# Perceiver block on one core: PE's second part inside both branches, and products of a constant ahead of five of its waits

## The chip, the cores and the metric

The kernel runs on one core of a Trainium2 chip. The metric is device time in microseconds (us) of one execution; before it is 1503.57 us, the median of three runs (1502.83 to 1508.02). The engines are PE (TensorE, with its weight loads shown as PEld), DVE (VectorE), ACT (ScalarE), POOL (GpSimd) and SP (SyncE, which here only issues DMAs). Each engine runs its own list of instructions in order, and the lists meet only through semaphores.

## The reference

A batch of 32 sequences of 64 tokens (2048 tokens, 256 features, kept transposed as x[feature, token]) goes through three residual steps:

```
x = x + cross_attention(layernorm(x), ctx, ctx, mask)   # 16 heads of 16, 1601 context rows per sequence
x = x + span_attention(layernorm(x))                    # 16 heads
x = x + ffn(layernorm(x))                               # a shared gated unit, and 8 experts, 2 for each token
```

The second step takes two numbers for each token and head from `h @ W_span.T`, a centre and a sharpness, and weighs the 64 positions with them:

```
mean = sigmoid(span[..., 0]) * m ;  soft = softplus(span[..., 1])
scores = -soft[..., None] * (pos - mean[..., None])**2
out = softmax(scores) @ (h @ W_val.T) ;  x = x + out @ W_out.T
```

The mask of this input holds ones only; the kernel must handle others too, for which it has a second version of part of its program.

## The kernel before

Each engine's program has three parts in a row. `queries` (the first 64 us) normalises x, projects the queries and prepares masks and weights. `cross_attention` runs over the 32 batches: in turn n PE computes scores and products of batch n and the keys, values and score maxima of batch n + 1. `tail` holds the rest: the output projection, the span step and the feed-forward step, over four chunks c of 512 tokens (8 sequences each), and then the routed experts.

**The branch.** The scores need an additional matmul for each tile if any mask element is 0. So PE's program of the turns exists twice. PE loads a number from the mask (`rows_all`, line 867) and compares it (line 868): `pe.If(rows_all < S)` holds `run(masked=True)`, a loop over the turns; `pe.Else()` holds `run(masked=False)`, all 31 turns written out, some 5,400 rows of PE's list. With a mask of ones the Else part runs. The other engines have no such branch.

**Head and body.** What PE does after the last turn is an order written out by hand, in two strings. `PE_HEAD` mixes the last batch's scores (`s0` to `s25`) and products (`p0` to `p10`, `l0`) with the first steps of the tail. `PE_BODY` holds all the others. A step is a letter and a chunk: `W` output projection of the cross attention (line 1417), `M`, `V` mean and variance of the first layernorm of the tail (lines 1449 and 1455, into `ln_bank[0]`), `m`, `v` those of the second, `S` the span product (line 1464, sixteen matmul records of 32 columns), `T` the turning of the packed span rows (line 1473), `A` one unit of distances (lines 1495, 1496), `X` values (1506), `U` sums (1514), `O` products (1523), `Z` output projection of the span step (1417 again), `F`, `G` the shared unit and `K`, `P` the experts (1531). `W0 W1 W2 M0 V0 S0 T0` stand in the head. `rest(pe)` returns both as functions: `rest_head` is called within `run`, in both branches, and `rest_body` once behind them.

**The waits that the change touches.** `S` for chunk c waits for `h_done`: ACT takes a logarithm from the bank (`lnv`, line 1143) and an exponential (1145), then DVE multiplies twice (`t_h`, line 1314). `V` waits for `sq_done`, ACT's square of what DVE has centred (`xc_done`, line 1303). `T` waits for `packed_done`, the end of nine dependent small DVE steps (lines 1325 to 1334) behind ACT's four on the span product. `mean_w` is a constant 128 x 128 tile (1/256 everywhere) made at the start; line 435 multiplies it with itself 18 times ahead of the first work.

**The start of batch 1.** In the first turn PE computes two chunks of keys of batch 1 (line 762), then scores of batch 0 (815), further keys, and score chunks of batch 1 (792). The last need the queries' rows of batch 1 (`qstack`, six DMAs of line 557) and a pair of its keys (`kstack`, line 564), all issued on SP's queue, there behind the load of the next context (545), which waits for the last `ctx_lo` of POOL (599).

Of the kernel before, what the change touches and what calls it, by code (L numbers as in the profile page):

```python
# [22 lines left out]
P = 128  # L23
B, S, S2, D = 32, 64, 1601, 256
# [416 lines left out]
def cross_attention(nc, sb, ins, bank, w, first_in, d, attn_out, out_done, q_parts, sem):  # L441
# [299 lines left out]
    def tensor(pe, early, rest):  # L741
# [60 lines left out]
        def scores(b, kt, h, masked):  # L802
            m = keys_of(kt)
            if kt == 0:
                pe.wait_ge(shift_done, 2 * b.n + h + 1)
                if h == 0 and isinstance(b.n, int) and b.n < 2:
                    pe.wait_ge(d["rows_in"][b.n], 16)

            need(pe, exp_done, NST * b.n + 2 * kt + h - 1)
            if masked:  # L810
                mask = w["mask_k"][0:m, kt, :].unsqueeze(1).to_broadcast([m, 2 * GROUPS, S])
                nc.tensor.matmul(st[h][0:m, :], w["ident_h"][0:m, 0:m], mask, start=True, stop=True, skip_group_check=True)
            for g in range(GROUPS):
                p = GROUPS * h + g
                mm = nc.tensor.matmul(st[h][0:m, g * PW:(g + 1) * PW], kstack[b.slot][0:KROWS, p, kt * P:kt * P + m],  # L815
                                      qstack[b.slot][0:KROWS, p, :], start=not masked and g == 0, stop=True, skip_group_check=True)
            mm.then_inc(st_ready, 1)
# [23 lines left out]
        def run(masked):  # L841
            def turn(cur, nxt, split, third):
                for kt in range(KT):
                    for what, i in slots[kt]:
                        if cur:
                            if what == "S":
                                scores(cur, kt, i, masked)
                            if what == "P":
                                products(cur, i)
                            if what == "L" and not first(cur):  # L850
                                products(before(cur), KT - 1)
                        if nxt:
                            if what == "K":
                                keys(nxt, i)
                            if what == "V":
                                values(nxt, i)
                            if what == "M":
                                chunk_scores(nxt, i)
                            if what == "T":
                                turn_shift(nxt)  # L860
            turns(pe, turn, loop=masked)
            rest_head({**last_products, "s": lambda i, _: scores(at(B - 1), i // 2, i % 2, masked)})


        rest_head, rest_body = rest(pe)
        last_products = {"l": lambda i, _: products(at(B - 2), KT - 1), "p": lambda kt, _: products(at(B - 1), kt)}
        rows_all = pe.value_load(w["rows_all"][0:1, 0:1], min_val=0, max_val=S)
        with pe.If(rows_all < S):
            run(masked=True)
        with pe.Else():  # L870
            run(masked=False)
        rest_body(last_products)

    return {"sync": sync, "vector": vector, "gpsimd": gpsimd, "scalar": scalar, "tensor": tensor}

# [12 lines left out]
def tail(nc, ins, bank, attn_out, out_done, wo, bo_all, mean_w, eps_col, ident, out_dram, d, sem):  # L888
# [6 lines left out]
    NC = NTOK // E  # L895
    FT = HS // P
    CLS = S // E

    PE_HEAD = """l0 s0 s1 s2 s3 p0 s4 s5 p1 s6 s7 p2 s8 p3 W0 s9 s10 s11 p4 s12 s13 M0 s14 s15 W1 s16 s17 V0 s18 s19 W2 S0 p5 p6 p7
        s20 p8 s21 s22 p9 s23 T0 s24 p10 s25"""  # L900
# [46 lines left out]
    with ExitStack() as own:  # L947
# [463 lines left out]
        def tensor(pe):  # L1411
            emitted = dict.fromkeys("WZFG", 0)

            def project(wt, src, done):
                for m in range(NK):
                    for k in range(NK):
                        i = nc.tensor.matmul(proj[m][:, :], wt[:, k, m * P:(m + 1) * P], src[k], start=k == 0, stop=k == NK - 1)
                i.then_inc(done, 1)
# [31 lines left out]
                i.then_inc(mean[j], 1)  # L1450

            def variances(c, j):
                pe.wait_ge(sq_done[j], c + 1)
                for k in range(NK):
                    i = nc.tensor.matmul(ln_bank[j][:, :], mean_w[:], sq[j][:, k, :], start=k == 0, stop=k == NK - 1)  # L1455
                i.then_inc(var[j], 1)

            def spans(c, _):
                if c == 0:
                    pe.wait_ge(s["w_in"], 4 * 16)  # L1460
                pe.wait_ge(s["h_done"], c + 1)
                for blk in range(BLOCKS):
                    for k in range(NK):
                        i = nc.tensor.matmul(ln_bank[0][:, 2 * H * blk:2 * H * (blk + 1)], h[c % 2][:, k, blk * P:(blk + 1) * P],
                                             wspan[:, k, :], start=blk == 0 and k == 0, stop=k == NK - 1, skip_group_check=True)
                i.then_inc(s["span"], 1)

            def turn_rows(c, _):
                if c == 0:
                    pe.wait_ge(s["turn_ready"], 2)  # L1470
                pe.wait_ge(s["packed_done"], c + 1)
                for blk in range(BLOCKS):
                    i = nc.tensor.matmul(ln_bank[0][:, blk * P:(blk + 1) * P], packed[:, blk, :], ident_r[:], start=blk == 0, stop=True,
                                         skip_group_check=True)
                i.then_inc(s["turned"], 1)
# [197 lines left out]
```

## Time and profile before

| what | value |
|---|---|
| median of three runs | 1503.57 us (1502.83 to 1508.02) |
| the profiled execution | 1506.76 us |
| its span, first to last instruction | 1504.9 us |
| busy: PE, PEld, DVE, ACT, POOL | 98%, 83%, 66%, 61%, 30% |
| mean granted clock of PE | 0.991 of 2.4 GHz |
| PE waited in S, T, V of line 1455 | 3.9, 2.2, 1.0 us |

The profile is of one execution. In order of time, a row gives the start, the duration, the engine, the line and what is written from what; behind it in brackets is the idle time of the engine before it and what released it, as inferred from semaphores. A row can gather several records of one kind. Durations of PE's records overlap, since matmuls are pipelined: the distance from one start to the next tells more than the duration. By stretch, the profile gives each engine's busy time and the granted clock, 1.00 for 2.4 GHz and 0.50 for 1.2 GHz.

### The profile page before, as it was taken

The page shows a single profiled execution, that of the slowest core. Times are in us where ns is not written, and L with a number is a line of the kernel's source. Part 1 is how long each engine was busy: PE and PEld are TensorE (multiplying, and loading weights), DVE is VectorE, ACT ScalarE, POOL GpSimd, SP SyncE. Part 2 cuts the span into 40 slices and gives each one's busy share as a digit, 9 for nine tenths or more (in the row PEclk, how much of TensorE's full clock was granted, in tenths as well). Part 3 has the DMA queues.
Part 4 walks back from the last instruction along what each step waited for, and adds up shares of the span by engine and source line. Part 5 has one row for each costly group of instructions (what it writes and reads, how often), then busy time and mean ns, then how long its engine had stood idle before and what let it go on. Part 6 is the DMA issues. An engine that isn't in the chain of part 4 may idle for free. (4 is left out here: it accounts for less than half of the span.)

```text
span 1504.9 us, 56291 instructions
## 1 busy us (share of the span) xinstructions
PE 1469.9 (98%) x23456; PEld 1251.7 (83%) x23456; DVE 1000.3 (66%) x3958; ACT 922.0 (61%) x1827; POOL 450.2 (30%) x564
## 2 busy tenths in 40 slices
PE   9899999999999999999999999999999999999999
PEld 5688888888888888888888888888888885555698
DVE  5766666676666677676676667666667774655436
ACT  4366666665666666666666666666666664689583
POOL 5433333333333333333333333333333303001143
PEclk9999999999999999999999999999999999899999
DMA  5634444444344444444444444444444333000012
GB/s 179 185 101 103 115 116 109 118 118 120 101 120 116 112 119 118 111 117 108 116 121 116 103 117 117 105 117 118 115 117 117 89 104 122 1 1 9 21 57 85
DMA packets 91758, 156.24 MB, mean 104 GB/s; under 512 B 44896, under 2 KB 55904, under 8 KB 91488
## 3 DMA queue, kind: packets, MB, share of 16 engines
q1 hardware_dynamic: 91216, 151.57, 37.3%
q8 instruction: 189, 3.10, 0.9%
q0 software_dynamic: 288, 1.05, 0.2%
q14 instruction: 65, 0.53, 0.1%
HBM read 69.61 MB, written 4.19 MB: 49 GB/s over the span
## 5 line engine op out<-in xcount | busy, mean ns | idle before, releaser
L682 DVE CUSTOM_DVE_ANT_0 junk<-bank,mask_q 128x400 bf16<-128x400 f32 (+1 forms) x1024 | 547.5, 571 | 178.0 <-issue 171.9
L627 ACT ACTIVATE probs<-bank 128x512 f32<-128x512 f32 (+1 forms) x832 | 468.3, 596 | 124.1 <-PE bank L815 115.3
L596 POOL CAST ctx_hi<-ctx_raw 128x400 fp32r<-128x400 f32 x248 | 123.0, 525 | 782.2 <-PE bank L772 782.2
L815 PE MATMUL bank<-qstack,kstack 104*128 104x128 f16 (+1 forms) x3328 | 289.1, 220 | 1.2 <-ACT probs L627 1.0
L772 PE MATMUL bank<-wv_hi,ctx_hi 128*128 128x256 f32 (+1 forms) x832 | 280.2, 337 | 0.0
L671 DVE SCALAR_TENSOR_TENSOR k_lo<-bank,bk,k_hi 128x400 f16<-128x400 f32 (+1 forms) x256 | 162.0, 633 | 161.6 <-ACT k_hi L637 161.5
L647 ACT ACTIVATE v<-bank 128x256 f32<-128x256 f32 (+1 forms) x416 | 159.6, 384 | 178.6 <-PE bank L772 172.3
L792 PE MATMUL bank<-kstack,qstack 96*128 96x400 f16 (+1 forms) x1024 | 266.9, 336 | 2.0 <-issue 1.3
L815 PEld LDWEIGHTS bank<-qstack,kstack 104*128 104x128 f16 (+1 forms) x3328 | 214.7, 99 | 61.3 <-issue 18.3
L637 ACT ACTIVATE k_hi<-bank,bk 128x400 f16<-128x400 f32 (+1 forms) x256 | 152.3, 595 | 177.9 <-PE bank L762 169.9
L599 POOL TENSOR_TENSOR ctx_lo<-ctx_raw,ctx_hi 128x400 fp32r<-128x400 f32 x248 | 253.6, 1043 | 0.0
L772 PE MATMUL bank<-wv_lo,ctx_hi 128*128 128x256 f32 (+1 forms) x832 | 233.4, 281 | 0.0
L772 PE MATMUL bank<-wv_hi,ctx_lo 128*128 128x256 f32 (+1 forms) x832 | 232.0, 279 | 0.0
L832 PE MATMUL bank<-probs,v 128*32 128x64 f32 x13312 | 221.6, 221 | 6.5 <-issue 5.9
L832 PEld LDWEIGHTS bank<-probs,v 128*32 128x32 f32 x13312 | 198.8, 110 | 21.6 <-issue 12.9
L762 PE MATMUL bank<-ctx_hi,wk_hi 128*128 128x400 f32 (+1 forms) x512 | 191.0, 373 | 4.6 <-POOL ctx_lo L599 4.5
L762 PE MATMUL bank<-ctx_hi,wk_lo 128*128 128x400 f32 (+1 forms) x512 | 177.3, 346 | 0.0
L762 PE MATMUL bank<-ctx_lo,wk_hi 128*128 128x400 f32 (+1 forms) x512 | 176.9, 345 | 0.0
L772 PEld LDWEIGHTS bank<-wv_hi,ctx_hi 128*128 128x128 f32 (+1 forms) x832 | 154.4, 186 | 5.7 <-issue 0.5
L772 PEld LDWEIGHTS bank<-wv_lo,ctx_hi 128*128 128x128 f32 (+1 forms) x832 | 154.4, 186 | 0.0
L772 PEld LDWEIGHTS bank<-wv_hi,ctx_lo 128*128 128x128 f32 (+1 forms) x832 | 153.5, 184 | 0.0
L792 PEld LDWEIGHTS bank<-kstack,qstack 96*128 96x128 f16 x1024 | 81.8, 98 | 48.1 <-issue 16.8
(172 smaller groups left out, 1642.0 us busy)
## 6 DMA issues: line engine op xcount, KB each, us to landing
ctx_raw<-in_ctxT SPq DMA_DIRECT2D x32, 1602.0 KB, 6.9
kstack<-k_hi SPq DMA_DIRECT2D x512, 100.1 KB, 2.2
kstack<-k_lo SPq DMA_DIRECT2D x256, 100.1 KB, 2.2
weight<-in_w SPq DMA_DIRECT2D x18, 256.0 KB, 2.7
x<-in_xT SPq DMA_DIRECT2D x8, 512.0 KB, 9.1
qstack<-q_parts SPq DMA_DIRECT2D x192, 16.0 KB, 5.2
out_yT<-y SPq DMA_DIRECT2D x8, 256.0 KB, 2.9
weight<-in_sw SPq DMA_DIRECT2D x3, 512.0 KB, 6.3
```

The source lines that it names most:

```text
L596: nc.gpsimd.tensor_copy(c_hi[:, k, s0:s0 + n], raw[:, k, s0:s0 + n]).then_inc(ctx_hi, 1)
L599: nc.gpsimd.tensor_tensor(c_lo[:, k, s0:s0 + n], raw[:, k, s0:s0 + n], c_hi[:, k, s0:s0 + n].bitcast(F32), ALU.subtract).then_inc(ctx_lo, 1)
L627: nc.scalar.activation(probs[kt % NP][0:m, GROUPS * h:GROUPS * (h + 1), :], st[h][0:m, :], ACT.Exp, scale=DK ** -0.5 / (UP * UP)).then_inc ...
L637: nc.scalar.activation(k_hi[:, t, s0:s0 + n], pj[(b.slot + c) % 2][:, 0:n], ACT.Identity, bias=w["bk"][:, t:t + 1]).then_inc(khi_done, 1)
L647: nc.scalar.activation(heads, pj[(b.slot + NCK + i) % 2][0:m, 0:D].rearrange("s (p e d) -> s p e d", e=2, d=DK), ACT.Copy).then_inc(v_done, 1)
L671: nc.vector.scalar_tensor_tensor(k_lo[:, t, s0:s0 + n], pj[(b.slot + c) % 2][:, 0:n], w["bk"][:, t:t + 1], k_hi[:, t, s0:s0 + n], ALU.add, ...
L682: nc.vector.tensor_tensor_reduce(junk[i % SM][:, 0:n], sm[i % SM][:, 0:n], w["mask_q"][:, s0:s0 + n], 1.0, -3.0e38, ALU.add, ALU.max, part ...
L762: mm = nc.tensor.matmul(o, w[wp][:, k, t * P:(t + 1) * P], cp[:, k, s0:s0 + n], start=i == 0, stop=i == len(terms) - 1)
L772: mm = nc.tensor.matmul(o, cp[:, k, j * P:j * P + m], w[wp][:, k, :], start=i == 0, stop=i == len(terms) - 1)
L792: nc.tensor.matmul(sm[i % SM][:, 0:n], qstack[b.slot][0:KSTACK, p, :], kstack[b.slot][0:KSTACK, p, s0:s0 + n], start=True, stop=True).then ...
L815: mm = nc.tensor.matmul(st[h][0:m, g * PW:(g + 1) * PW], kstack[b.slot][0:KROWS, p, kt * P:kt * P + m], qstack[b.slot][0:KROWS, p, :], sta ...
L832: mm = nc.tensor.matmul(ob[32 * g:32 * g + 32, t * S:(t + 1) * S], v[b.slot][0:m, kt, c0:c0 + 2 * DK], probs[kt % NP][0:m, p, S * e:S * (e ...
```

## The change

Three things, all on PE. `rest_body` moves from behind the two branches into `run`, so that both branches hold head and body. The branches are exchanged: the comparison is now `rows_all == S`, with the unmasked program first and the masked one in the Else. And a table `KEEP` puts products of `mean_w` with itself, 128 columns each, ahead of five waits: 7 before span product S0, 4 before variance V1 (chunk 1 of the first norm), 9 before T1, 3 before S2 and 6 before S3. They write into a bank that is free there and that the awaited step writes next (for T into `proj[1]`), and each is preceded by a wait of its own that makes the bank free.

```diff
             rest_head({**last_products, "s": lambda i, _: scores(at(B - 1), i // 2, i % 2, masked)})
+            rest_body(last_products)
...
-        with pe.If(rows_all < S):
+        with pe.If(rows_all == S):
+            run(masked=False)
+        with pe.Else():
             run(masked=True)
-        with pe.Else():
-            run(masked=False)
-        rest_body(last_products)
...
+    KEEP = {("S", 0): 7, ("V", 1, 0): 4, ("T", 1): 9, ("S", 2): 3, ("S", 3): 6}
...
+            def keep_going(where, dst):
+
+                for _ in range(KEEP.get(where, 0)):
+                    nc.tensor.matmul(dst[:, 0:P], mean_w[:], mean_w[:], start=True, stop=True)
...
             def variances(c, j):
+                if ("V", c, j) in KEEP:
+                    pe.wait_ge(xc_done[j], c + 1)
+                    keep_going(("V", c, j), ln_bank[j])
                 pe.wait_ge(sq_done[j], c + 1)
...
             def spans(c, _):
...
+                if ("S", c) in KEEP:
+                    pe.wait_ge(lnv[0], c + 1)
+                    keep_going(("S", c), ln_bank[0])
                 pe.wait_ge(s["h_done"], c + 1)
...
             def turn_rows(c, _):
...
+                if ("T", c) in KEEP:
+                    proj_free(1)
+                    keep_going(("T", c), proj[1])
                 pe.wait_ge(s["packed_done"], c + 1)
```

PE's list around the branch before, as laid out in memory. The first rows behind the comparison are the masked program (its line 812 is the additional matmul); the unmasked one begins behind the jump of line 868:

```order
L800 MATMUL bank<-turn_down,row_max 8x128
L867 TENSOR_LOAD rows_all
L867 ISA x2
L868 COMPARE_AND_BRANCH
```

```order
L812 MATMUL bank<-mask_k,ident_h 65x512
L815 MATMUL bank<-qstack,kstack 65x128 x4
L868 UNCONDITIONAL_BRANCH
L762 MATMUL bank<-ctx_hi,wk_hi 128x400
L762 MATMUL bank<-ctx_hi,wk_lo 128x400
L762 MATMUL bank<-ctx_lo,wk_hi 128x400
```

And now, where the row behind the comparison belongs to the unmasked program, and the jump at that program's end leads over the masked one:

```order
L868 TENSOR_LOAD rows_all
L868 ISA x2
L869 COMPARE_AND_BRANCH
L762 MATMUL bank<-ctx_hi,wk_hi 128x400
L762 MATMUL bank<-ctx_hi,wk_lo 128x400
```

```order
L1546 MATMUL bank<-gelu_lo,w_0_hi 128x256
L1546 MATMUL bank<-gelu_hi,w_0_lo 128x256
L869 UNCONDITIONAL_BRANCH
L762 MATMUL bank<-ctx_hi,wk_hi 128x400
L762 MATMUL bank<-ctx_hi,wk_lo 128x400
```

So the target of the taken path moved from some 1,700 rows away to the next row, and the far jump from the start to the end.

PE around S0 before (in the unmasked program; 1417 is W2, 1464 the span product, 832 the products of batch 31):

```order
L1455 MATMUL bank<-t_sq,mean_w 128x512 x2
L815 MATMUL bank<-qstack,kstack 128x128 x8
L1417 MATMUL bank<-attn_out,wo 128x512 x4
L1464 MATMUL bank<-wspan,t_h 128x32 x8
L832 MATMUL bank<-probs,v 32x64 x48
```

and now (1423 is W2, 1418 the constant products, 1476 the span product):

```order
L1464 MATMUL bank<-t_sq,mean_w 128x512 x2
L815 MATMUL bank<-qstack,kstack 128x128 x8
L1423 MATMUL bank<-attn_out,wo 128x512 x4
L1418 MATMUL bank<-mean_w 128x128 x7
L1476 MATMUL bank<-wspan,t_h 128x32 x8
L832 MATMUL bank<-probs,v 32x64 x48
```

Nothing else stands in a new place there; seven rows came in between W2 and S0. The same holds at T1, before:

```order
L1495 MATMUL bank<-rows,sel_a 128x512
L1496 MATMUL bank<-rows,sel_b 128x512
L1473 MATMUL bank<-ident_r,packed 128x128 x4
L1495 MATMUL bank<-rows,sel_a 128x512
L1496 MATMUL bank<-rows,sel_b 128x512
```

and now, with nine products between the two units A0 and T1 (line 1488):

```order
L1510 MATMUL bank<-rows,sel_a 128x512
L1511 MATMUL bank<-rows,sel_b 128x512
L1418 MATMUL bank<-mean_w 128x128 x9
L1488 MATMUL bank<-ident_r,packed 128x128 x4
L1510 MATMUL bank<-rows,sel_a 128x512
L1511 MATMUL bank<-rows,sel_b 128x512
```

A row here is one matmul of the program; the trace shows two records for a plain float32 one, hence sixteen for S. PE's list has one more change: the body, some 780 rows, stands in both branches, so the masked program moved and the whole is that much longer.

## Rows read from the trace of the kernel before

**Rows 1.** The page, section 1: busy us, share of the span, instructions.
```profile
PE 1469.9 (98%) x23456; PEld 1251.7 (83%) x23456; DVE 1000.3 (66%) x3958; ACT 922.0 (61%) x1827; POOL 450.2 (30%) x564
```

**Rows 2.** PE in order of time: start us, us, engine, line, work.
```profile
68.37 0.67 PE L762 MATMUL bank<-ctx_hi,wk_hi 128*128 128x400 f32 x1 [4.47 <-POOL ctx_lo L599]
...
80.59 0.68 PE L792 MATMUL bank<-kstack,qstack 96*128 96x400 f16 x3
```

**Rows 3.** PE's sequencer, line 868: the branch; ns, and its start.
```profile
L868 PEldq COMPARE_BRANCH  x1: 3824/3824/3824, 64.4 to 64.4; - x1
```

**Rows 4.** DMA queues in 63 to 69 us: packets, MB, share.
```profile
q8 instruction: 1, 0.02, 1.0%
```

**Rows 5.** One stretch: us; PE, PEld, DVE, ACT, POOL busy; clock; DMA.
```profile
65.14:71.97 6.83, 3.60 (x11) 3.60 (x12) 0.59 (x2) 0.59 (x1) 4.22 (x5) 0.50 0.41 136
```

**Rows 6.** The SP queue, 68 to 77 us, and the last landings of L557.
```profile
68.44 3.61 SPq L557 DMA_DIRECT2D qstack<-q_parts  x6
76.56 0.51 SPq L564 DMA_DIRECT2D kstack<-k_hi  x1
...
DMA to landing us min/median/max: 4.4/4.6/4.7
```

**Rows 7.** Four stretches of the end; columns as in rows 5.
```profile
1263.22:1270.04 6.82, 6.82 (x154) 6.02 (x157) 2.43 (x10) 2.98 (x8) 0.00 (x0) 0.50 0.09 29
...
1287.11:1293.94 6.83, 5.24 (x11) 3.35 (x12) 4.24 (x13) 4.81 (x10) 0.00 (x0) 0.50 0.00 0
...
1307.59:1311.00 3.41, 3.41 (x7) 1.65 (x6) 3.13 (x11) 1.88 (x5) 0.00 (x0) 0.50 0.00 0
...
1331.48:1334.90 3.42, 3.42 (x95) 3.35 (x98) 0.00 (x0) 2.21 (x6) 0.00 (x0) 0.50 0.02 7
```

**Rows 8.** PE in order of time, 1262 to 1300 us; columns as in rows 2.
```profile
1262.14 2.61 PE L1464 MATMUL bank<-wspan,t_h 128*128 128x32 f32 x16 [1.77 <-DVE t_h L1314]
...
1264.68 2.79 PE L832 MATMUL bank<-probs,v 128*32 128x64 f32 x96
...
1271.54 0.65 PE L832 MATMUL bank<-probs,v 128*32 128x64 f32 x32
...
1272.38 1.94 PE L1449 MATMUL bank<-x,mean_w 128*128 128x512 f32 x4
...
1276.78 1.99 PE L1455 MATMUL bank<-t_sq,mean_w 128*128 128x512 f32 x4 [0.96 <-ACT t_sq L1136]
...
1288.70 1.11 PE L1473 MATMUL bank<-ident_r,packed 128*128 128x128 f32 x4 [2.08 <-DVE packed L1334]
...
1291.43 3.13 PE L1449 MATMUL bank<-x,mean_w 128*128 128x512 f32 x4
```

**Rows 9.** PE, continued, 1302 to 1345 us.
```profile
1302.59 1.99 PE L1523 MATMUL bank<-attn_out,vbd 128*32 128x64 f32 x128 [0.34 <-ACT vbd L1193]
1305.20 1.97 PE L1464 MATMUL bank<-wspan,t_h 128*128 128x32 f32 x16 [0.62 <-DVE t_h L1314]
...
1308.38 4.90 PE L1417 MATMUL bank<-rs,wout 128*128 128x512 f32 x8
...
1330.19 2.47 PE L1464 MATMUL bank<-wspan,t_h 128*128 128x32 f32 x16 [1.48 <-DVE t_h L1314]
1332.59 3.07 PE L1523 MATMUL bank<-attn_out,vbd 128*32 128x64 f32 x128
...
1341.02 3.67 PE L1417 MATMUL bank<-rs,wout 128*128 128x512 f32 x8
```

**Rows 10.** Products of the constant with itself, 128 columns, at the start.
```profile
1.56 5.33 PE L435 MATMUL bank<-mean_w 128*128 128x128 f32 x24
...
7.11 0.98 PEld L435 LDWEIGHTS bank<-mean_w 128*128 128x128 f32 x8
```

**Rows 11.** Who waited on PE, and PE's sequencer at the block's end.
```profile
PE bank L832 <- issue: 5.9, 6, 1.4
...
L156 PEldq DRAIN  x1: 2345/2345/2345, 1499.2 to 1499.2; - x1
```

## The prediction, made before the changed kernel ran

> **What bounds the kernel now.** I read the page first: PE is busy for 1469.9 us of 1504.9 [rows 1]. Such a share says that PE sets the pace, not that it runs well: a matmul at half clock is busy too. So the next two views were PE in order of time (where does it stand idle?) and the busy time by stretch, whose clock column is what the throttle granted. In both the reader is to look at the same two places, because the long middle (batches 1 to 31, from the first scores to batch 31) has next to no idle time on PE, full clock, and no line of this diff but its place in memory.
>
> The first place is the branch. After PE's last instruction of the first part it stands idle for 4.47 us [rows 2]. The row names POOL's ctx_lo as the releaser. I don't believe it: the first keys product waits for the first chunk's ctx_lo of batch 1, and POOL splits the chunks in order, so it was the last chunk, not the first, that ended just then. The sequencer's row has the cause: the compare and branch of line 868 starts at 64.4 us and takes 3.824 us [rows 3], and one block of instructions (0.02 MB) is fetched meanwhile [rows 4]. In the kernel before, the masked part stands first and this input (a mask of ones) jumps over it. PE then comes back at half clock: 0.50, the 1.2 GHz level, from 65.14 to 71.97 us [rows 5].
>
> The second place is the end. Four stretches, of 6.8, 6.8, 3.4 and 3.4 us, run at 0.50 [rows 7]. Each begins at, or a microsecond or a few after, one of the waits of this diff: the span product S0 after 1.77 us idle, T1 (packed rows) after 2.08 [rows 8], S2 after 0.62 and S3 after 1.48 [rows 9]. Ahead of each fall stood idle time and the sixteen 32-column matmuls of a span product. V1 waits 0.96 us [rows 8] with no fall behind it.
>
> **Part 1, the branch turned round.** PE's instructions stay the same; the unmasked part now follows the comparison directly. Removed: a jump of 3.82 us. What a comparison that falls through costs, no row shows; it lies between nothing and the same 3.82 us. I take 0.1, since what the long row holds is the fetch, and the block that follows needs none that isn't under way. So PE could start its keys at about 64.7 rather than 68.37, and as it stood idle for 0.8 us only, at full clock: of the half-clock stretch, 3.6 us were work [rows 5], which shrink to about 1.8. That is 3.7 + 1.8 = 5.5 us at the end of the first keys.
>
> It isn't kept whole. The first score chunk of batch 1 ran at 80.59 [rows 2] and would now be due at 75.1. It needs the queries' rows, six DMAs issued on SP from 68.44 to 72.05, of which the last lands 4.7 us after its issue, at 76.3 [rows 6]. Their start hangs on POOL's last ctx_lo, which the change doesn't touch. Behind them on the same queue comes the first pair's k_hi: it was issued at 76.56, when its keys were done; now its keys are done at 71, it goes out at 72.1, and its three DMAs end about 77. So the new wait is on this chunk, some 1.9 us, and 80.59 becomes about 77.1: **3.5 us gained** (bounds: none, if falling through costs like the jump, and 5.5). From there PE sets the pace again.
>
> The Trainium skill (Runtime: NRT & Kernel Launch, section Instruction fetch mechanics) says that a taken branch to a target outside the fetched window waits for a DMA of that page, and the trace agrees: 3.824 us and one fetch. By Advanced Engine Details and Errata of the Trainium skill, section Control Flow Timing, a compare-and-branch is about 108 ns; by that figure the sum would be the same within 0.1 us.
>
> The same cost comes back at the end: the unmasked part now closes with a jump over the masked one. PE's sequencer runs ahead of its matmuls; it entered the drain at 1499.2 and waited there for 2.345 us [rows 11]. A jump of 3.8 us started then is over at 1503.0, ahead of the span's end at 1504.9, which the last store sets. So I cost it at nothing, with some 1.9 us of cover; without any cover it costs 3.8. The jump at the old join goes; no idle time stands there, so it gives nothing.
>
> **Part 2, the constant products.** Twenty-nine products mean_w times mean_w, 128 columns, two matmul records each. The kernel already issues 18 such at its start: records at the first, slow pace take 5.33/24 = 0.22 us, those at the later pace 0.98/8 = 0.12 with the tail, about 0.112 without [rows 10]. A product costs 0.22 us at full clock and 0.43 at half. So S0 gets 7 x 0.22 = 1.6 us in a wait of 1.77, V1 0.9 in 0.96, T1 2.0 in 2.08, S2 0.7 in 0.62, S3 1.3 in 1.48: 6.5 us in 6.9, each about as long as its wait. At full clock they cost nothing: the cover is the idle time, and what ends it (t_h, packed, t_sq) comes from DVE and ACT. The waits put ahead of them are on events long past: the logarithm for S, the centred chunk for V, the free bank for T. Nothing is queued behind them that could have gone earlier, as PE is in order.
>
> What they bring is the clock. If it stays at 2.4 GHz through all four stretches, the gain is the work in them at full pace, each compared with the same form at full clock:
> - A (S0): the span product 2.61 against 1.97 us, the three products of batch 31 2.79 against 3 x 0.65 [rows 8, 9], and some 2.6 us of smaller pieces to about 1.5: 0.6 + 0.85 + 1.1 = 2.6.
> - B (T1): the means 3.13 against 1.94; T1 and two units, 1288.70 to 1291.43, to about 1.7 [rows 8]: 2.2. The next centring stands behind 16 small bias steps on DVE, so I take 2.0 (1.2 to 2.5).
> - C (S2): the output projection 4.90 against 3.67 [rows 9]: 1.3 with the units.
> - D (S3): 2.47 against 1.97, and 3.07 against 1.99 [rows 9]: 1.5.
>
> Sum 7.4 us. No wait is expected to take its place: within A to D, DVE and ACT wait for PE, and what follows up to the end is PE's shared and routed products, which just start earlier.
>
> **The sum.** The profiled execution took 1506.8 us (span 1504.9 and 1.9 around it), 3.2 above the median of the runs. 1506.8 - 3.5 - 7.4 = 1495.9. If the 3.2 us are the profile's cost, it would be 1492.7; if the median run had fewer half-clock stretches, they aren't there to be won and 1495.9 stands. I take **1495.0**. One more unknown: moved code meets other block boundaries. PE's six idle pieces ahead of line 832 with no releaser, 5.9 us [rows 11], look like late fetches in dense small matmuls; they can come out 2 us either way.
>
> **Rivals.**
> 1. The clock falls all the same (17%). For it: the sixteen 32-column matmuls behind each wait stay, and V1 shows that idle time alone doesn't decide. Against: idle time stood ahead of all four falls. It gives 1503.6 - 3.5 = 1500.1, up to 1503. The Trainium skill (TensorE: Matmul & The Clock Gate, section Why this matters for your kernels) warns only of idle gaps longer than any of these; by that rule filling them would give nothing, which is this rival. The trace disagrees: the clock fell behind gaps of 0.62 to 2.08 us.
> 2. Falling through costs what the jump did (10%): 1495.0 + 3.5 = 1498.5.
> 3. Slower (5%): the products themselves run at half clock. Place: S0 to S3, if the clock has fallen before PE gets there. Price: 29 x 0.43 = 12.4 us against 6.9 of waits, 5.5 over; from 19 products at half clock on they outlast the waits by more than the start gives back. With the end jump uncovered as well: 1503.6 + 5.5 + 3.8 - 3.5 = 1509.4.
>
> **How the numbers follow.** Both gains hold: 68%, 1490.5 to 1499. Under 0.5%, 7.5 us, a measurement of this kernel can't be told from no change; the border is 1496.05. Of the 68, 57 lie under it; 3 more come from rivals 1 and 2 with the other part larger: faster 0.60. Slower by over 0.5% needs rival 3 nearly whole: 0.03. The rest is 0.37. The range 1490 to 1500.5 takes in the 68, rival 2 and the best part of rival 1.
>
> **What would show it.** Line 869's branch in well under 0.5 us; the first score chunk at 76.5 to 77.5 behind a wait of 1 to 2.5 us; clock 1.00 at 65 us and from 1260 to 1335; M1's means start about 6 us earlier than 1272.4; a fetch behind the end jump that ends ahead of the last store. Wrong would be: 3.8 us at the fall-through, 0.50 behind S0 or T1, or products that end after t_h.

## The result: no gain, and the profile after

| | before | changed |
|---|---|---|
| median | 1504.28 us (20 runs, 1497.8 to 1511.7) | 1509.42 us (20 runs, 1504.5 to 1513.5) |
| ratio, 95% interval | 1 | 1.0024 (1.0013 to 1.0036) |
| profiled execution, span | 1506.76, 1504.9 us | 1508.69, 1506.9 us |
| mean granted clock, profiled / mean of runs | 0.991 / 0.994 (35 later runs) | 0.996 / 0.996 |

Forecast were 1495.0 us and a range of 1490 to 1500.5. The mechanisms that the forecast named came as it said, and yet the kernel is 0.24% slower: a small loss, but clear of its interval.

Page of the changed kernel, section 1, to be read beside [rows 1], and the branch on PE's sequencer (ns, first and last start), beside [rows 3]:

```profile
PE 1472.2 (98%) x23514; PEld 1254.3 (83%) x23514; DVE 999.8 (66%) x3958; ACT 920.8 (61%) x1827; POOL 450.5 (30%) x564
...
L869 PEldq COMPARE_BRANCH  x2: 88/1890/3693, 64.6 to 1500.8; - x2
```

The comparison that falls through takes 88 ns at 64.6 us; the far jump, 3693 ns, now stands at 1500.8. PE in order of time, beside [rows 2] (start us, us, engine, line, work, idle time before it):

```profile
64.89 0.42 PE L762 MATMUL bank<-ctx_hi,wk_hi 128*128 128x400 f32 x1 [0.73 <-issue]
...
77.36 0.67 PE L792 MATMUL bank<-kstack,qstack 96*128 96x400 f16 x3 [1.65 <-DMA qstack<-q_parts]
```

The first keys start at 64.89 rather than 68.37, the first score chunk of batch 1 at 77.36 rather than 80.59 (77.1 was forecast), behind the new wait for the queries' rows (1.65 us, forecast 1.9).

Stretches of the changed kernel by busy time and clock, columns as in [rows 5]:

```profile
78.73:82.14 3.41, 3.41 (x105) 3.19 (x107) 0.59 (x5) 1.03 (x3) 0.00 (x0) 0.50 0.70 161
1239.26:1242.67 3.41, 3.41 (x76) 2.76 (x68) 2.73 (x6) 1.72 (x4) 1.74 (x3) 0.50 1.01 364
1263.22:1270.04 6.82, 6.81 (x207) 5.97 (x207) 3.86 (x12) 4.11 (x11) 0.00 (x0) 1.00 0.15 42
1287.11:1293.94 6.83, 6.52 (x28) 3.52 (x32) 4.89 (x20) 5.24 (x13) 0.00 (x0) 1.00 0.00 0
...
1368.96:1372.37 3.41, 3.41 (x6) 1.45 (x6) 3.37 (x6) 2.54 (x4) 0.00 (x0) 0.50 0.00 0
```

The four half-clock stretches of [rows 7] are gone. Three shorter ones are new: one right behind the new wait, one at 1239 us, one at 1369 us. (Three kernels among the experiments have one at 1238 to 1240 us too, with and without the products; what brings it stays open.) The constant products fill their waits (line 1418), and what follows runs at full pace, beside [rows 8]:

```profile
1261.80 1.72 PE L1418 MATMUL bank<-mean_w 128*128 128x128 f32 x14
1263.48 1.97 PE L1476 MATMUL bank<-wspan,t_h 128*128 128x32 f32 x16
1265.38 1.55 PE L832 MATMUL bank<-probs,v 128*32 128x64 f32 x96
...
1287.18 0.66 PE L1488 MATMUL bank<-ident_r,packed 128*128 128x128 f32 x4
...
1289.02 1.96 PE L1455 MATMUL bank<-x,mean_w 128*128 128x512 f32 x4
```

What came on top is in the list of who waited, beside [rows 11] (us in total, times, longest; "issue" is idle time for which the profile shows no releaser), and in PE's order at the first O product, beside [rows 9]:

```profile
PE bank L832 <- issue: 5.9, 6, 1.8
PE bank L1538 <- issue: 4.7, 4, 1.7
...
PE bank L762 <- issue: 1.7, 2, 1.0
PE bank L792 <- DMA qstack<-q_parts: 1.6, 1, 1.6
...
PE bank L792 <- issue: 1.5, 3, 0.7
```

```profile
1300.17 1.95 PE L1538 MATMUL bank<-attn_out,vbd 128*32 128x64 f32 x122 [0.90 <-ACT vbd L1194]
1303.80 0.31 PE L1538 MATMUL bank<-attn_out,vbd 128*32 128x64 f32 x6 [1.68 <-issue]
```

An O product is 128 small matmuls that wait once, at their start. Now PE stands still six matmuls before the end of it, for 1.68 us, released by nothing that the profile shows. The DMA view of 1300 to 1304 us (40 slices of 0.1 us) has a single packet, an instruction block, which begins in the slice of 1301.4 us, 2.4 us before PE goes on:

```profile
DMA  0000000000000050000000000000000000000000
...
q8 instruction: 1, 0.02, 1.4%
```

I then numbered all of PE's records from the start of the trace, its loads and those of its sequencer included (a semaphore wait is a record too; without them the pattern is lost), and looked at each idle piece without a releaser in the middle (from 76 us on) and in the O products. In the kernel before, 7 of 10 stand at remainder 144 or 145 of 256, in the changed one 7 in the middle and all 4 in the O products at 193 or 194; these end 2.2 to 2.9 us after a fetch has begun. The others, at line 792, stand at other remainders and end 3.2 to 3.7 us behind a fetch. There are 189 fetches of 16384 bytes for 48,047 records, one for every 256. I read the pieces at one remainder as block boundaries whose block isn't there yet.

Start times of the changed kernel less those of the profiled kernel before, record by record: -3.2 us at 80.6, -1.7 at 83.8 (half clock), -3.9 at 420, +0.5 at 1212, +1.6 at 1256, -1.5 at 1272 (S0), -2.4 at 1302 (T1), -0.4 at 1305 (late fetch in O0), -2.2 at 1313 (S2), -3.2 at 1341 (S3), 0.0 at 1376 (late fetch in O2 and the half clock behind it), +1.5 at 1405 (O3), +2.0 at the end. So this execution lost 3.3 us in the middle (83.8 to 1256 us) and gained nothing from there on, where 7.4 us were forecast.

### The profile page after: what moved, and what is told of

Its sections match the earlier page's. It is cut to its first block and busy times, and to the rows that moved or that the text cites. A ratio compares the mean times of both kernels' runs of the same rounds, so it can differ in the third digit from the quotient of the medians.

```text
span 1506.9 us, 56408 instructions
## 1 busy us (share of the span) xinstructions
PE 1472.2 (98%) x23514; PEld 1254.3 (83%) x23514; DVE 999.8 (66%) x3958; ACT 920.8 (61%) x1827; POOL 450.5 (30%) x564
```

## The experiments

The theory, called P (placement) from here: the change moved code in memory, and late instruction blocks in PE's dense small matmuls ate what branch and clock gave. The rivals: the gains weren't there, or the products or the end jump cost time. Each ratio is against the kernel before on the same chip. "Place" in the table is the remainder of 256 at which the middle's late fetches stand, counted over the records that all kernels share; the middle's idle time is that without a releaser ahead of lines 762, 772, 792 and 832, in the one profiled execution, without two pieces of another kind: 0.7 us behind the branch in the changed kernel and e10, and 0.6 us that is left of the wait for the queries' rows in e6. O0 to O3 are the O products of chunks 0 to 3.

| run | ratio, 95% interval | mean clock | place | idle, middle | idle, O |
|---|---|---|---|---|---|
| before | 1 | 0.994 | 144 | 7.2 | 0 |
| changed | 1.0024 (1.0013 to 1.0036) | 0.996 | 193 | 8.4 | 4.7 |
| e1 | 0.9995 (0.9977 to 1.0012) | 0.998 | 77 | 11.1 | 0 |
| e2 | 1.0050 (1.0035 to 1.0065) | 0.992 | 77 | 10.8 | 0 |
| e3 | 0.9987 (0.9971 to 1.0004) | 0.995 | 193 | 7.4 | 0 |
| e4 | 1.0012 (0.9997 to 1.0028) | 0.996 | 117 | 8.5 | 0 |
| e5 | 0.9992 (0.9980 to 1.0004) | 0.998 | 193 | 7.6 | 0 |
| e6 | 0.9975 (0.9963 to 0.9987) | 0.999 | 165 | 5.0 | 0 |
| e7 | 1.0028 (1.0014 to 1.0042) | 0.996 | 193 | 7.3 | 4.8 |
| e8 | 0.9997 (0.9984 to 1.0009) | 0.997 | 144 | 7.1 | 0 |
| e9 | 1.0008 (0.9993 to 1.0023) | 0.995 | 144 | 10.8 | 1.6 |
| e10 | 1.0020 (1.0007 to 1.0032) | 0.996 | 193 | 5.9 | 1.9 |
| e11 | 1.0003 (0.9987 to 1.0019) | 0.998 | 165 | 6.8 | 0 |
| e12 | 1.0002 (0.9990 to 1.0015) | 0.999 | 153 | 8.9 | 0 |
| e13 | 0.9955 (0.9940 to 0.9971) | 0.999 | 165 | 6.1 | 0 |
| e14 | 0.9988 (0.9973 to 1.0004) | 0.997 | 144 | 5.7 | 0 |
| e15 | 0.9979 (0.9968 to 0.9991) | 0.998 | 193 | 5.5 | 0 |

**e1, the changed kernel with other places.** 29 small products (116 records) ahead of the branch.

```diff
+        for _ in range(29):
+            nc.tensor.matmul(ob[0:32, 0:S], w["turn_down"][:, 0:32], w["turn_down"][:, 0:S], start=True, stop=True)
         rows_all = pe.value_load(...)
```

> The changed kernel with 29 tiny products (32 x 64 columns, four records each, 116 in all, about 1 us) between the last step of the first part and the load of rows_all. They do no work that is needed. They lie ahead of the wait of the first score chunk of batch 1, which was 1.65 us, so they should cost nothing. Theory P (placement): in the traces of before and after, PE's idle pieces without a releaser lie, counted in PE's executed records, all at one remainder of 256: 144 before, 193 after, and end 2.3 to 2.9 us behind the fetch of an instruction block. After pays 4.7 us of them within the four O steps, before none. 116 records more bring the remainder to 77: the O stalls go (4.7 to under 0.5 us), the half-clock stretch behind O2 at 1369 us (1.3 us) with them, the middle stays at 9 to 10 us of stalls. So 5 to 6 us below the changed kernel, equal to or up to 2 us under before. Rival R (the constant products or the exchanged branches cost it elsewhere): as the changed kernel, or 1 us slower by the added products.

The O products have no idle piece left and the median is 1502.77 us, 0.3% under the changed kernel by the ratios. The middle was worse (one piece of 3.2 us at 1242 us, half clock there). The 29 products took 3.4 us, not 1; they push the keys into the new wait, and there is no half clock behind it here. So e1 changes two things at once, and the O products alone are for e5 and e15.

**e2, dead code alone.** The kernel before with 17 small products (68 records) at the head of the masked program, which never runs.

```diff
         with pe.If(rows_all < S):
+            for _ in range(17):
+                nc.tensor.matmul(ob[0:32, 0:S], w["turn_down"][:, 0:32], w["turn_down"][:, 0:S], start=True, stop=True)
             run(masked=True)
```

> The kernel before with 17 tiny products (68 records) at the head of the masked branch, which this input never executes; it stands ahead of the unmasked one in memory. Every executed instruction is as before, 68 places further on. Theory P: the remainder goes from 144 to 76, a block boundary then falls 200 to 250 records into each of the four O steps (their first records are at 124, 84, 84 and 123): about 4 us of stalls there, and the middle goes from 7.4 to about 9.3 us. In sum 4 to 6 us slower than before. Rival R: dead code costs nothing, the time is that of before.

Who waited on PE in e2:

```profile
PE bank L832 <- issue: 8.4, 7, 2.1
...
PE bank L792 <- issue: 1.8, 4, 0.6
```

1510.46 us, 1.0050. The late fetches moved from remainder 144 to 76 and 77, by the 68 records. PE executes the same instructions; that places alone move the time is thereby shown. But the 4 us that were expected in the O products didn't come: they have no idle piece. By the start differences of its profiled execution the loss lies in the middle: -0.1 us at 83.8, +7.0 at 1256. Of that, 3.6 us are idle time; two half-clock stretches at 1162 and 1247 us, each right behind a late fetch, can be most of the rest. e1, at the same place, lost 7.0 us in the middle as well.

**e3 and e4, one part of the change each.** e3 is the changed kernel with `KEEP = {}`; e4 the kernel before with `KEEP` and its three `if ... in KEEP` blocks.

> The changed kernel without any constant product (an empty table). Theory P: the start keeps its 3.2 us, the middle loses 2.5 (9.9 against 7.4 us of stalls), one half-clock stretch behind the first score chunk of batch 1 costs 1.3, the remainder 193 meets no O step at its end (they start at 124, 84, 84, 123), and the four half-clock stretches of before are back. So within 1.5 us of before, 3 to 5 us below the changed kernel. Rival R1 (the exchanged branches are what costs): as the changed kernel or slower, as the clock's gain of 7.6 us is gone: 1511 to 1516.

> The kernel before with the constant products alone: branches in the old order, the second part behind them. Theory P: PE's start is as before (3.8 us in the branch), the middle keeps its 7.4 us of stalls and remainder 144; the clock stays at 1.00 from 1260 to 1335 us, which brings 7 us or so; the O steps now start at 204, 200, 200, 239, so that the boundary at 144 lies 161 to 200 records into them, where a stall of 0 to 1 us each is possible. In sum 3 to 7 us faster than before. Rival R2 (the products are the loss): 2 to 5 us slower than before.

e3 held in kind: the branch alone gives 0.9987, 2 us, a little more than expected (its interval reaches 1.0004), and far from a loss through the exchanged branches. e4 missed: the products alone give nothing in the median, although its profiled execution (span 1499.7) shows all four stretches at full clock. The seven products of S0 stand in the masked program too, so the place moved by 28 records, to 117, and the middle's idle time rose from 7.2 to 8.5 us. That left the clock term open. Neither has an idle piece in the O products: the loss needs both parts of the change.

e3 shows more. Its profiled execution has no product in any wait, and still its clock stayed at 1.00 at S0 and S2, behind waits of 1.07 and 0.62 us; it has two half-clock stretches from 1260 to 1340 us (1286 and 1327), 3.4 us each, where the profiled kernel before has four with 20.5 us.

**e5, only the O products moved.** The changed kernel, with T1's nine products replaced by five and 29 small ones, which puts all behind T1 100 records further on.

```diff
-    KEEP = {..., ("T", 1): 9, ...}
+    KEEP = {..., ("T", 1): 5, ...}
...
                     keep_going(("T", c), proj[1])
+                    for _ in range(29):
+                        nc.tensor.matmul(proj[1][0:32, 0:64], mean_w[:, 0:32], mean_w[:, 0:64], start=True, stop=True)
```

> The changed kernel, with only the place of the tail's code moved: ahead of T1 stand 5 constant products of 128 columns and 29 of 64 columns by 32 in place of the 9, so everything behind T1 lies 100 matmul and load records further on in PE's list; nothing ahead of it moves. Placement theory (the four idle pieces of the O products are fetches of instruction blocks that come late because a block boundary falls 210 to 249 records into each O): the boundary now falls some 110 to 149 into each, the idle time within them goes from 4.7 us to under 0.5, the middle's idle pieces stay at one record in 256 as in the changed kernel, and the median is 3 to 6 us under the changed kernel's, 1.000 to 1.002 of the kernel before. Rival (the O products wait for data, values or unit sums that the constant products delay): the 4.7 us stay within 1 us and the time with them, 1.0024 or more.

The idle 4.7 us are gone and the ratio falls from 1.0024 to 0.9992, by 4.8 us (3 to 6 expected). The O products didn't wait for data. Nor did this filler come free. PE around T1 in e5:

```profile
1281.90 1.28 PE L1418 MATMUL bank<-mean_w 128*128 128x128 f32 x10
1283.10 3.43 PE L1487 MATMUL bank<-mean_w 128*32 128x64 f32 x58
1286.46 0.66 PE L1490 MATMUL bank<-ident_r,packed 128*128 128x128 f32 x4
```

4.5 us of products stand in a wait of 2.1: T1 starts 2.3 us late by start differences. This overrun sits in e5, e6, e8, e11 and e12 alike.

**e6, the new wait filled too.** e5 and seven products of `turn_down` with itself ahead of the first score chunk of batch 1.

```diff
+            if i == 0 and isinstance(b.n, int) and b.n == 1:
+                need(pe, *((shift_done, 2 * b.n) if SHIFT_BANK == 0 else (sm_done, NMX * b.n)))
+                for _ in range(7):
+                    nc.tensor.matmul(sm[0][:, 0:P], w["turn_down"][:], w["turn_down"][:], start=True, stop=True)
             if i == 0:
                 pe.wait_ge(qstack_in[b.slot], 16 * QSTACK_DMAS * b.used)
```

> The kernel of the run before, and 7 products of a constant (128 columns) in the wait ahead of the first score chunk of batch 1. If the half-clock stretch at 78.7 us in the changed kernel comes from the new wait of 1.65 us, the clock stays at 1.00 there and the run gains a further 1 to 1.5 us of it; the middle's code lies 28 records further on, so its idle pieces come elsewhere, 2 us either way. Expected 0.996 to 1.001 of the kernel before. If the stretch comes whatever is in the wait, it is there again and the products cost up to 0.3 us.

No half clock at 78 us, and from 80.6 to 83.8 us nothing is lost, where the changed kernel loses 1.5 us; ratio 0.9975. The middle's place moved too, which e11 takes apart.

**e7, the end jump.** The changed kernel without `with pe.Else(): run(masked=True)`; the masked program is left out.

> The changed kernel without its masked program (which this input never runs; masks with zeros would be computed wrongly), so the jump at the end of PE's program leads to the next row instead of far ahead. What is executed ahead of the jump stays at its place. If the end jump of 3.69 us is covered, as the prediction had it, the time is that of the changed kernel within 1.5 us, with the same idle pieces at record 193 of 256. If the run's end waits for it, it is 2 to 3.7 us faster (0.998 to 0.9995 of before where the changed kernel is 1.0024).

```profile
L869 PEldq COMPARE_BRANCH  x1: 87/87/87, 62.6 to 62.6; - x1
```

The jump of 3.7 us is gone, and the ratio is 1.0028, no faster than with it: the jump was covered. The late fetches stayed, in the O products too (4.8 us).

**e8, e4 with the places held.** e4 with T1 as in e5 and 57 small products (228 records) of dead code, so that 28 + 228 = 256.

> The kernel before with the constant products alone (five waits, T1 filled as in the first run of this group), the branch as it was, and with 228 records of code that never runs put into the masked program, so that the middle's block boundaries fall at the same records as in the kernel before (144 of 256; 117 in the run with the products alone) and those of the O products at 80 to 130 records into each. Placement theory: the products' gain by the clock stands alone, the mean granted clock goes from 0.994 to 0.996 or 0.997, the median is 2.5 to 4.5 us under the kernel before, ratio 0.997 to 0.9985, and the middle's idle pieces are those of the kernel before (7 us). Rival (the products cost as much as the clock gives, since they outlast their waits): ratio 1.000 to 1.002, as with the products alone.

The place is 144 again, as meant. At 0.9997 the gain of 0.0015 to 0.003 was missed, and the overrun at T1 explains 2.3 us of it.

**e9 and e10, how sharp the distance is.** e9 is the kernel before with 17 small products ahead of T1, e10 the changed kernel with two more there.

> The kernel before, with 17 products of 64 columns by 32 (68 records) executed ahead of T1, inside its wait of 2.08 us, and nothing else: the middle stays at its place (idle pieces at record 144 of 256), and the block boundaries fall 208, 248, 248 and 209 records into the four O products instead of 20, 60, 60, 21. Placement theory: idle pieces of 0.2 to 1.7 us come up inside the O products, 3 to 5 us in sum, where the kernel before has none, and the median is 2 to 5 us above it (1.0015 to 1.0035). Against it stands the run with 68 records of dead code, whose O products have the same distances to a boundary and no idle piece: if the distance alone doesn't decide, there is none here either and the time is that of the kernel before within 1 us.

> The changed kernel with two more small products (8 records) ahead of T1. The boundaries fall 237, 241, 241 and 202 records into the O products instead of 245, 249, 249, 210. If the late fetch is a matter of tens of records, the four idle pieces stay, 4 to 5 us in sum, at record 193 of 256, and the time is the changed kernel's within 1 us; if a few records decide whether a fetch starts ahead of the O product's wait or behind it, one or more of them is gone and the time is 1 to 4 us less.

e9 has one idle piece, in O2, and none in the three other O products, and 1.0008 where 1.0015 to 1.0035 was expected:

```profile
1368.30 1.98 PE L1527 MATMUL bank<-attn_out,vbd 128*32 128x64 f32 x124 [1.15 <-ACT vbd L1193]
1371.86 0.31 PE L1527 MATMUL bank<-attn_out,vbd 128*32 128x64 f32 x4 [1.58 <-issue]
```

So a boundary late in an O product makes the stall possible in the kernel before as well, but doesn't decide it. e10 lost two of its four for 8 records. In e2 the O products stand at the same distances as in e9, and their fetches began 0.9 to 2 us before the O products of chunks 1 to 3 started; in the changed kernel those that stalled them began 0.6 to 1.3 us after the start of chunks 0, 2 and 3. When a fetch begins relative to the wait ahead of it decides; what sets that moment stays open. e10's time fell by less (0.0004) than its 2.8 us of idle time; the intervals overlap, so its share isn't settled.

**e11 and e12, the fastest kernel taken apart.** e11 is e5 with seven small products ahead of the branch (e6's places, without its products at batch 1); e12 is e6 with three small ones there.

> The first run of the second group (the changed kernel with its O products shifted, 0.9992) with 7 small products (28 records) ahead of the branch, so that the code stands at the same places as in the fastest run so far (0.9975), but nothing fills the wait ahead of the first score chunk of batch 1. If the 2.1 us between those two came from the clock kept at 78 us, this one has a half-clock stretch there and a median 1 to 2 us above the fastest, 0.9985; if they came from the place of the middle's code, its idle pieces are 5 to 6 us here too and it is within 0.7 us of the fastest.

> The fastest kernel so far (changed kernel, O products shifted, 7 constant products ahead of batch 1's first score chunk) with 12 more records ahead of the branch: the middle's idle pieces then come at content 12 records earlier. Nothing that computes is changed. Placement theory: the idle pieces change in size and places, 5.3 us to anything from 4.5 to 10 us, and the time with their sum; ratio 0.9965 to 1.0005. Rival (the sum of idle pieces varies from run to run by as much, and place says nothing for so small a step): within 0.7 us of the fastest.

e11 has a half-clock stretch of 6.8 us at 76.4 us behind a wait of 3.5 us, and 1.0003 where 0.9985 was expected: direction right, size not; its stretch is twice as long as the changed kernel's and costs 2.6 us by start differences. e12 ran with mean clock 0.999 and yet gives 1.0002; its middle has 3.9 us more idle time than e6's. Three profiled executions at place 165 have 5.0, 6.8 and 6.1 us, e12's at 153 has 8.9. At one place the sum varies too, at 144 from 5.7 to 10.8 (the latter in e9, whose profiled execution is its slowest of twelve, 1511.9 us at a median of 1505.2), so one profile doesn't settle 12 records.

**e13 to e15, a filler that fits.** T1 gets four products of 128 columns and 50 of a cheaper form (one matmul record each instead of two), 116 records in all: in e13 on top of e6, in e14 on top of e8, in e15 on top of the changed kernel.

```diff
+    KEEP = {..., ("T", 1): 4, ...}
...
+                    for _ in range(50):
+                        nc.tensor.matmul(proj[1][0:32, 0:32], ident_r[:, 0:32], ident_r[:, 0:32], start=True, stop=True)
```

> The fastest kernel so far (changed kernel, O products shifted, 7 constant products ahead of batch 1's first score chunk; 0.9975) with a cheaper filler ahead of T1: 4 constant products of 128 columns and 50 single-pass products of 32 columns (116 records) in place of 5 and 29 double-pass ones, which took 4.5 us in a wait of 2.1. The O boundaries fall 137 to 141 and 102 records in. If the overrun of 2.3 us at T1, seen in five traces, is real, T1 starts as early as in the changed kernel, and the median is 2 to 2.5 us lower, ratio 0.995 to 0.997. If T1 waits on something else, it stays 0.9975.

> The kernel before with the constant products alone and places held (0.9997 with the expensive filler), now with the cheap one ahead of T1. It gives the price of the prediction's second term by itself: if the clock's gain is there and the filler ate it, ratio 0.997 to 0.999 and mean granted clock 0.997; if the term was mis-sized for a median run, which has a clock of 0.994 where the profiled one had 0.991, it is at the upper end of that, 0.998 to 0.999; if the products give nothing at all, 0.9995 or more.

> The changed kernel with nothing but its O products shifted, by the cheap filler (80 records; boundaries 165, 169, 169, 130 records in). The price of the four late fetches by themselves: expected 4.7 us less idle and no cost at T1, ratio 0.9965 to 0.9985 against 1.0024 for the changed kernel. If the changed kernel loses elsewhere, 0.9985 or more.

PE in e15, around T1 and at O0:

```profile
1280.68 1.05 PE L1418 MATMUL bank<-mean_w 128*128 128x128 f32 x8
1281.49 1.81 PE L1487 MATMUL bank<-ident_r 128*32 128x32 f32 x50
1283.15 0.64 PE L1490 MATMUL bank<-ident_r,packed 128*128 128x128 f32 x4
...
1295.93 1.99 PE L1540 MATMUL bank<-attn_out,vbd 128*32 128x64 f32 x128 [0.91 <-ACT vbd L1194]
```

The filler ends within 0.25 us of its wait, and O0's 128 matmuls run in one piece. All three came out as expected: e15 0.9979, e14 0.9988, e13 0.9955. e13 is 1497.15 us where the kernel before is 1503.81; by its ratio it beats both kernels. Its stretches from 76 to 80 and from 1262 to 1335 us (busy time, clock):

```profile
76.00:80.00 4.00, 3.74 (x146) 3.33 (x147) 1.58 (x9) 1.37 (x3) 0.00 (x0) 1.00 0.68 156
...
1262.00:1335.00 73.00, 71.09 (x731) 46.50 (x728) 43.73 (x104) 55.39 (x118) 0.00 (x0) 1.00 0.01 2
```

## Why the prediction was wrong, step by step

**The step that failed** is the last of the sum: "they can come out 2 us either way". It read the 5.9 us ahead of line 832 rightly as late fetches, but took the places in the middle for the only ones. The O products have none in [rows 9] and so had no row. They are 256 records in 2 us, as dense as line 832's. The turned branch moved the boundaries from 144 to 193, and the constant products push the O products along: 28 records from S0, 16 from V1, 36 from T1 and more behind. In O0 the boundary thereby moved from about 20 records in to about 245, close to its end. One part of the change alone leaves it at about 69 (e3) or 168 (e4), where no O product stalled. The term measured: 4.7 us idle in the O products, and 1.5 us by the half-clock stretch behind the stall, at 1369 us; the four executions that stalled in O2 (changed, e7, e9, e10) are the four that have a stretch there. By ratios the same kernel with these products moved (e15) is 1.0024 - 0.9979 = 0.0045, 6.8 us, faster, and at least 3.3 by the ends of the two intervals. In the traces the start differences from 1256 us to the last matmul are -7.4 us in e1, e13, e14 and e15, -7.5 in e4, and 0.0 in the changed kernel: 7.4 us. The middle doesn't show a share: at place 193 it idled 5.5 to 8.4 us in six executions, at 144 5.7 to 10.8 in four, and from 83.8 to 1256 us the start differences are -0.7 to +3.3 us (mean 1.8) in the six, -1.6 to +7.3 (mean 2.0) in the four. So the 3.3 us that the profiled execution lost there are within what one place gives.

This term isn't the whole miss. Without it the kernel would be at 0.9979, about 1501.1 us, still above the range's end of 1500.5. The gains forecast were 8.6 us, and 3.2 came (e15); the term that was too large is part 2's, below. The sign that it had named, M1's means about 6 us earlier than 1272.4, came as 1.5 us in the changed kernel, after the 3.3 us lost in the middle, and as 5.8 in e15.

**Part 1, the branch, was right.** 88 ns for the fall-through, 3.22 us at the first score chunk of 3.5, and the end jump covered (e7), though it starts 1.6 us later than thought, at 1500.8, and ends at 1504.5, ahead of the span's end at 1506.9. Left out was that the new wait brings a fall of the clock, as the waits of the end did: 1.5 us, from -3.2 to -1.7 at 83.8. e3, the branch alone, gives 2.0 us (0.9987). In e6, e12 and e13, with that wait filled, nothing is lost from 80.6 to 83.8 us. What the first part gives varies as well: the comparison starts anywhere from 62.6 to 64.9 us in the profiled executions without added products ahead of it, the two compared here at 64.4 and 64.6.

**Part 2, the clock, was right in the trace and too large for a median run.** By start differences A to D gave 3.1, 0.9, 1.8 and 1.1 us, 6.9 of 7.4; in e13 3.4, 1.1, 1.7 and 1.6. B is half of what was forecast; I didn't test why. But alone, with places held, the products give 1.8 us of median (e14, 0.9988, interval to 1.0004). One reason is in the clocks: (1 - 0.991) x 2 x 1505 = 27 us at half clock in the profiled execution, (1 - 0.9937) x 2 x 1502 = 19 in a mean run of the kernel before (0.989 to 0.998 in 35 runs). The prediction weighed that and took its profiled execution as the base all the same. With about 7 us of each at the branch, 12 instead of 20.5 us were there to be won at the end, some 4.3 us instead of 7.4 (an estimate). The traces say the same without that estimate: e2 and e3, which have no product in any wait, run the stretch from 1256 us to the last matmul 4.4 and 4.5 us faster than the profiled kernel before. Of the 7.4 us only 2.9 to 3.0 are left for the products against these two. The products themselves can cost a little: against the work ahead of it, S0 starts 0.3 to 0.5 us later than in e3, and the cheaper filler delays T1 by 0.2. The rest of the way to 1.8 lies within e14's interval.

**The rivals.** Rival 1 (the clock falls all the same) didn't come: 1.00 in all four stretches. The Trainium skill (TensorE: Matmul & The Clock Gate, section Why this matters for your kernels), which warns of longer gaps only, was rightly set aside. Of the 13 profiled executions with the products, 12 have no half-clock stretch from 1260 to 1340 us (e7 has one, behind a late fetch in O0), where the kernel before has four, e2 three, e3 two and e9, with a filler at T1 alone, one. Rival 2 is excluded by 88 ns. Rival 3 was the only case given that ends slower and nearly met the time, 1509.4 forecast and 1509.42 measured, but for a wrong reason: the products ran at full clock and the jump was covered. A number that fits doesn't confirm its mechanism.

**How far it adds up.** Branch alone -2.0 us (e3), products alone -1.8 (e14), sum -3.8; both with the O products moved -3.2 (e15). These agree, but the intervals of e3 and e14 just take in 1. The changed kernel is at +3.6; the 6.8 us between the last two is the price of the late fetches in the O products by definition, and the traces' 7.4 (or 4.7 + 1.5 = 6.2, counted piece by piece) is the check on it. With the first wait filled as well: -6.8 us (e13), though e13 also has the middle at another place.

## What to carry to other kernels

Small matmuls issued faster than a block of instructions arrives depend on where the block boundaries fall, and every instruction added in front, dead code too, moves them: number all records of the engine, the sequencer's too, take the remainder, and look at each dense group behind the edit, those above all that have no idle time now. Treat a gain under 0.5% on such a kernel as unproven until a variant with shifted code confirms it, and try shifts for their own sake. One profiled execution is one draw: here it had 27 us at half clock where a mean run has 19, so read a clock term from several before pricing it. A wait that a change creates needs the same filling as the old ones, and a filler has to be timed against its wait.

## What the runs showed of the hardware that was not expected

- 68 records of code that never runs cost 0.5% (e2). The Trainium skill (Runtime: NRT & Kernel Launch, section Instruction fetch mechanics) states that the next block is fetched while the present one executes, and that crossing a block's boundary is mostly hidden. Here most crossings are hidden too (7 to 16 idle pieces for 187 to 190 fetches in a trace), but some stall PE, those in dense small matmuls above all, for 0.2 to 3.2 us each, 5 to 13 us in a run.
- A taken far jump took PE's sequencer 3.3 to 4.3 us in 16 cases over all traces, the same comparison falling through 0.09 in eleven.
- Waits of 1.6 to 3.5 us of PE were followed by half-clock stretches of 3.4 or 6.8 us (at 78.7 us in the changed kernel, at 76.4 in e11); the 0.6 us left at the same place in e13 weren't.
- 29 products of 64 columns by 32, two matmul records each, took 3.4 us (e5); 50 of 32 columns by 32, one record each, took 1.8 (e15).
